# First pieces loaded in one go, and attention rows of the tail turned by VectorE instead of TensorE

## The reference

```python
x  = inputs                                  # (4, 1024, 256)
xn = layernorm(x)
# attention: 16 heads; the reshape takes heads along the sequence, then q, k, v are split
qkv = xn @ W_qkv + b_qkv                     # 256 -> 768
attn = softmax(mask(q @ k.T * 512 ** -0.5))
sa  = (attn @ v).reshape(4, 1024, 256)
out = sa @ W_out + b_out
# light network on every row: hidden 128; h = rms_norm(xn) * gamma_light
light = gelu(h @ w1_light + b1_light) @ w2_light + b2_light
# router: 50 iterations of coordinate descent on s = xn . routing_token, then top 256 of each batch
sel = top_k(exp((s + a + b) / 0.1), 256)
heavy[sel] = (gelu(rms_norm(xn[sel]) * gamma_heavy @ w1_heavy + b1_heavy) @ w2_heavy + b2_heavy) * gate
return x + out + light + heavy
```

## Time and profile before

| | before |
|---|---|
| median of 3 runs | 711.55 us (711.24 to 713.2) |
| profiled execution | 714.09 us, span 712.4 us |
| PE busy | 667.8 us (94%) |
| VectorE busy | 554.8 us (78%) |
| ScalarE busy | 403.5 us (57%) |
| GpSimd busy | 380.6 us (53%) |
| mean granted clock of PE | 0.982 |

### The profile page before, as it was taken

The page is one execution under the profiler, slowest core; times in us unless marked ns, Lnnn a source line. Parts: engine busy times, 40 slices in busy tenths (PEclk is TensorE's granted clock), DMA queues, the critical chain, the costliest instruction groups (busy, mean ns, idle before and its releaser), DMA issues. The chain is left out here.

```text
span 712.4 us, 12474 instructions
## 1 busy us (share of the span) xinstructions
PE 667.8 (94%) x3987; PEld 296.2 (42%) x3987; DVE 554.8 (78%) x1571; ACT 403.5 (57%) x908; POOL 380.6 (53%) x774
## 2 busy tenths in 40 slices
PE   4997999899999999899989999999999999999995
PEld 2653555333323333233323332333333436568665
DVE  4865888999999999999989999999998575152111
ACT  2332222787777777467768877777767554332320
POOL 4686130488775847857957853554442454413303
PEclk9999999999999999979999999999999999999998
DMA  8888996678949649696987944844833323442512
GB/s 276 207 219 196 242 264 179 154 141 129 180 70 161 129 63 163 103 132 111 152 160 99 164 73 52 120 75 51 174 63 29 121 60 92 147 148 88 119 59 30
DMA packets 247057, 92.49 MB, mean 130 GB/s; under 512 B 212992, under 2 KB 232608, under 8 KB 243872
## 3 DMA queue, kind: packets, MB, share of 16 engines
q1 hardware_dynamic: 245456, 89.60, 63.0%
q0 software_dynamic: 1536, 2.10, 1.8%
HBM read 56.65 MB, written 35.01 MB: 129 GB/s over the span
## 5 line engine op out<-in xcount | busy, mean ns | idle before, releaser
L1288 DVE CUSTOM_DVE_ANT_0 ps<-ps,maskrow 128x640 f32<-128x640 f32 (+7 forms) x512 | 375.3, 779 | 30.9 <-PE ps L1039 29.4
L897 ACT ACTIVATE strips<-ps 128x512 f32<-128x512 f32 (+1 forms) x608 | 313.2, 576 | 112.0 <-PE ps L1081 89.5
L1039 PE MATMUL ps<-QTk,QTq 96*128 96x512 bf16 (+3 forms) x768 | 189.2, 335 | 18.5 <-DVE mx L1288 10.6
L1081 PE MATMUL ps<-QTq,QTk 99*128 99x512 bf16 (+3 forms) x768 | 185.4, 331 | 2.8 <-DMA QTq<-m_d 1.9
L1099 PE MATMUL ps<-strips,vext 128*32 128x512 f32 (+3 forms) x1536 | 162.8, 500 | 0.9 <-DVE oT L1311 0.4
L1039 PEld LDWEIGHTS ps<-QTk,QTq 96*128 96x128 bf16 x768 | 53.3, 98 | 166.6 <-DVE mx L1288 133.1
L1081 PEld LDWEIGHTS ps<-QTq,QTk 99*128 99x128 bf16 x768 | 68.2, 98 | 89.3 <-ACT strips L897 41.2
L1739 POOL TENSOR_SCALAR_AFFINE_SELECT strips<-strips 128x512 f32<-128x512 f32 x128 | 79.3, 636 | 43.2 <-ACT strips L897 42.8
L999 PE MATMUL ps<-shared,xrT 128*128 128x384 f32 (+1 forms) x256 | 94.8, 503 | 0.2
L1288 DVE DVE_READ_ACCUMULATOR2_ANT mx<- 128x1 f32 x512 | 72.1, 141 | 0.0
L999 PEld LDWEIGHTS ps<-shared,xrT 128*128 128x128 f32 x256 | 47.3, 196 | 26.8 <-issue 3.1
(11 more groups left out here) (153 smaller groups left out, 689.8 us busy)
## 6 DMA issues: line engine op xcount, KB each, us to landing
pieces_d<-pieces SPq DMA_DIRECT2D x64, 192.0 KB, 3.4
qk<-qkv_d SPq DMA_DIRECT2D x64, 128.0 KB, 4.0
qkv_d<-shared SPq DMA_DIRECT2D x16, 384.0 KB, 3.8
QTq<-pieces_d SPq DMA_DIRECT2D x16, 384.0 KB, 5.2
QTk<-pieces_d SPq DMA_DIRECT2D x16, 384.0 KB, 7.7
vext<-qkv_d SPq DMA_DIRECT2D x16, 256.0 KB, 5.8
QTq<-pieces_d SPq DMA_DIRECT2D x16, 256.0 KB, 5.6
QTk<-pieces_d SPq DMA_DIRECT2D x16, 256.0 KB, 8.3
```

Source lines behind the costliest of these rows:

```text
L897: nc.scalar.activation(dst, src, ACT.Exp, scale=SCALE).then_inc(exp_done, 1)
L1039: mm = pe.matmul(psM[:, s, at:at + n], QTq[0:W, f % 3, c * 1024 + qb * P:c * 1024 + (qb + 1) * P], QTk[0:W, f % 3, c * 1024 + k0:c * 1024 ...
L1081: mm = pe.matmul(psE[:, (NE * q + j) % ES, k * n:(k + 1) * n], QTk[0:W + 3, q % 3, c * 1024 + kb * P:c * 1024 + (kb + 1) * P], QTq[0:W + 3 ...
L1288: ins = nc.vector.tensor_tensor_reduce(scores, scores, maskrow[:, 1024 - n:1024], 1.0, MASKED, ALU.add, ALU.max, mx[:, f % 2, 8 * c + qb:8 ...
```

## The change

It has two parts that don't touch each other.

In the projection, the transfers of the blocks' rows and pieces and of other data are put behind other tiles. Block 0's two piece loads are issued back to back; block 1's rows are loaded behind tile 10 instead of 5, its turn is at tile 13 instead of 10; block 2's turn is at tile 18 instead of 15; the value loads and the light weights are placed elsewhere.

In the tail, the attention rows are turned by VectorE (`turned`) in blocks of 32 x 32, two operations a unit, each of 128x512. A new view `sa_blocks` loads a unit's rows in four transfers with 256-byte rows, such that 32 x 32 blocks suffice, and W_out is loaded in the matching order of rows. `saT` holds a whole unit, twice. PE's transposes and ScalarE's copies go; `psC` has four banks; PE waits for a unit's turn at its first tile. On VectorE units (0, 0) and (0, 1) are turned ahead of the last item `("OT", 15, 1)`, and unit (i + 1, u) behind the evictions of unit (i, u) or soon after. In the heavy rows bias times gate is computed ahead (`heavy_bias`), and one operation is left behind the matmuls.

```diff
-    T_AT = {5: 0, 10: 1, 15: 2}
+    T_AT = {5: 0, 13: 1, 18: 2}
...
-                if t in (2, 5, 11, 16):
-                    load_qk((2, 5, 11, 16).index(t))
-                elif t in (4, 13):
-                    load_v(t // 10)
-                elif t == 20:
+                if t in (2, 10, 14, 20):
+                    load_qk((2, 10, 14, 20).index(t))
+                elif t in (26, 27):
+                    load_v((26, 27).index(t))
+                elif t == 16:
                     load_light()
-                elif t in (6, 15, 22):
-                    store_pieces((6, 15, 22).index(t))
-                elif t in (8, 17, 23):
-                    load_pieces((8, 17, 23).index(t), 0)
-                elif t in (9, 18, 24):
-                    load_pieces((9, 18, 24).index(t), 1)
+                elif t in (6, 17, 23):
+                    store_pieces((6, 17, 23).index(t))
+                elif t == 8:
+                    load_pieces(0, 0)
+                    load_pieces(0, 1)
+                elif t in (19, 24):
+                    load_pieces((19, 24).index(t) + 1, 0)
+                elif t in (21, 25):
+                    load_pieces((21, 25).index(t) + 1, 1)
...
+                for a in range(4):
+                    sp.dma_start(wout[32 * a:32 * a + 32, :, :], W_out.rearrange("(a k p) n -> a p k n", a=4, p=32)[a]
+                                 ).then_inc(wd_in, 16)
...
+            sa_blocks = sa_d.rearrange("(n m s) (a f) -> n a s m f", m=16, s=32, a=4)
...
-                sp.dma_start(sa_in[:, u], sb3[bass.ds(2 * i + u, 1)].rearrange("a p t e -> (a p) t e")).then_inc(c_in[u], 16)
+                for a in range(4):
+                    sp.dma_start(sa_in[32 * a:32 * a + 32, u].rearrange("p t e -> p (t e)").rearrange("p (m f) -> p m f", m=16),
+                                 sa_blocks[2 * i + u, a]).then_inc(c_in[u], 16)
...
-                o = psC[:, t % 2, 0:E]
+                o = psC[n % 4][:, 0:E]
...
+                if t == 0:
+                    pe.wait_ge(saT_done, KE * (2 * i + u + 1))
                 for k in range(KE):
-                    mm = pe.matmul(o, saT[:, t % 2, k * P:(k + 1) * P], wout[:, k, :], start=False, stop=(k == KE - 1))
+                    mm = pe.matmul(o, saT[u][:, k, t * P:(t + 1) * P], wout[:, k, :], start=False, stop=(k == KE - 1))
...
+            def turned(i, u):
+                dve.wait_ge(c_in[u], 16 * 4 * (i + 1))
+                if i > 0:
+                    dve.wait_ge(o_ps, 8 * (i - 1) + 4 * u + 4)
+                elif u > 0:
+                    dve.wait_ge(qk_ps, NE * NQ)
+                blocks = sa_in[:, u].rearrange("p t e -> p (t e)").rearrange("p (m k f) -> p k m f", k=KE, f=32)
+                for k in range(KE):
+                    nc.vector.transpose(saT[u][:, k, :].rearrange("p (m s) -> p m s", s=32), blocks[:, k]).then_inc(saT_done, 1)
+
+            last_outputs = ("OT", NQ - 1, 1)
             for item in order["Vector"]:
+                if item == last_outputs:
+                    turned(0, 0)
+                    turned(0, 1)
...
+            def heavy_bias(sts):
+                for st in sts:
+                    nc.vector.tensor_scalar(hv[:, st, :], bias_h, gw[:, st:st + 1], None, ALU.mult).then_inc(hb_done, 1)
...
-                    nc.vector.tensor_tensor(hv[:, st, :], psH[:, st % 2, 0:E], bias_h, ALU.add).then_inc(hv_half, 1)
-                    dve.wait_ge(hv_half, st + 1)
-                    nc.vector.tensor_scalar(hv[:, st, :], hv[:, st, :], gw[:, st:st + 1], None, ALU.mult).then_inc(hv_done, 1)
+                    nc.vector.scalar_tensor_tensor(out=hv[:, st, :], in0=psH[:, st % 2, 0:E], scalar=gw[:, st:st + 1],
+                                                   in1=hv[:, st, :], op0=ALU.mult, op1=ALU.add).then_inc(hv_done, 1)
...
             unit(0, 1, range(2, 4))
+            turned(1, 0)
+            turned(1, 1)
             gathered_invert(1)
             unit(1, 0)
+            turned(2, 0)
             gathered_normalise(1)
             gathered_gates()
             unit(1, 1)
+            turned(2, 1)
...
             unit(2, 0)
+            turned(3, 0)
             heavy_rows(range(2, 4))
             unit(2, 1)
+            turned(3, 1)
```

More of the change, by code:

```diff
@@ L386, in layer_kernel @@
     FIRST_DONE = FRONT_FROM + 2 * NU
-    T_AT = {5: 0, 10: 1, 15: 2}
+    T_AT = {5: 0, 13: 1, 18: 2}
     P_AT = {t + 2: f for t, f in T_AT.items()}
-    N_DCONST, N_CONST, N_FOLD = 2, 14, 5
+    N_DCONST, N_CONST, N_FOLD, N_WD = 2, 14, 5, 10
     N_SEARCH = 3
@@ L414, in layer_kernel @@
         psO = ps[:, 7]
-        psX = ps[:, 0:2]
         psG = ps[:, 6:8]
@@ L418, in layer_kernel @@
         psA = [ps[:, 4 + 2 * u:6 + 2 * u] for u in range(2)]
-        psC = ps[:, 4:6]
+        psC = [ps[:, b] for b in (0, 1, 4, 5)]
         psH = ps[:, 2:4]
@@ L536, in layer_kernel @@
         xgT = QTk[:, 0, :].bitcast(F32).rearrange("p (k n) -> p k n", k=KE)
-        saT = strips[:, 8192:8704].rearrange("p (b e) -> p b e", b=2)
+        saT = [y.rearrange("p (k n) -> p k n", k=KE) for y in (k_free[:, 3072:4096], QTq[:, 0, :].bitcast(F32)[:, 0:1024])]
         hot = [y.bitcast(BF16).rearrange("p (t n) -> p t n", n=NUM_HEAVY)
@@ L597, in layer_kernel @@
         h_done = sem("h_done")
-        saT_ps = sem("saT_ps")
         saT_done = sem("saT_done")
@@ L615, in layer_kernel @@
         ho_ps = sem("ho_ps")
-        hv_half = sem("hv_half")
+        hb_done = sem("hb_done")
         hv_done = sem("hv_done")
@@ L761, in load_bulk @@
                     sp.wait_ge(qkv_st[u], 16 * (NT // 4))
-                for dst, src in ((w2l, w2_l), (wout, W_out.rearrange("(k p) n -> p k n", p=P)),
+                for a in range(4):
+                    sp.dma_start(wout[32 * a:32 * a + 32, :, :], W_out.rearrange("(a k p) n -> a p k n", a=4, p=32)[a]
+                                 ).then_inc(wd_in, 16)
+                for dst, src in ((w2l, w2_l),
                                  (w2h, w2_h.rearrange("(k p) n -> p k n", p=P)),
@@ L832, in unit @@
                 if more:
-                    sp.wait_ge(saT_ps, 8 * i + 4 * u + 4)
+                    sp.wait_ge(saT_done, KE * (2 * i + u + 1))
                     load_sa(i + 1, u)
@@ L926, in hidden @@
                 nc.scalar.activation(hT[:, u, :], xrT[:, 0, 512 * (2 * i + u):512 * (2 * i + u) + 512], ACT.Gelu, bias=b1l[:, 0:1]).then_inc(h_done, 1)
[L928 to L937, removed]
             def gathered(h):
@@ L953, in _ @@
             hidden(0, 0)
-            unit(0, 0)
-            unit(0, 1)
+            hidden(0, 1)
             gathered(0)
+            hidden(1, 0)
             heavy_hidden(0, range(4))
-            unit(1, 0)
+            hidden(1, 1)
             heavy_hidden(0, range(4, NHC))
-            unit(1, 1)
+            hidden(2, 0)
             act.wait_ge(gu_done, 2 * NSLOT + 1)
             nc.scalar.activation(gscore[:, :], gu[:, :], ACT.Exp, scale=1.0 / EPS_ROUTE).then_inc(gs_done, 1)
-            unit(2, 0)
-            unit(2, 1)
+            hidden(2, 1)
             gathered(1)
+            hidden(3, 0)
             heavy_hidden(1, range(4))
-            unit(3, 0)
+            hidden(3, 1)
             heavy_hidden(1, range(4, NHC))
-            unit(3, 1, more=False)
         @block.tensor
@@ L1122, in _, with project_c @@
                     ring_item(item)
-            def transposes_c(i, u, t):
+            def project_c(i, u, t):
                 n = 8 * i + 4 * u + t
+                o = psC[n % 4][:, 0:E]
                 if t == 0:
[L1128 to L1132, removed]
+                    pe.wait_ge(h_done, 2 * i + u + 1)
+                if n == 0:
                     for x in slots[-MS:]:
@@ L1135, in transposes_c, with unit @@
                         pe.wait_ge(free[s], at + 1)
-                for k in range(KE):
[L1137 to L1141, removed]
-                o = psC[:, t % 2, 0:E]
[L1143 to L1155, removed]
-                    mm = pe.matmul(o, saT[:, t % 2, k * P:(k + 1) * P], wout[:, k, :], start=False, stop=(k == KE - 1))
+                    pe.wait_ge(wd_in, 16 * N_WD)
+                elif n == 2:
+                    pe.wait_ge(exp_done, NE * NQ)
+                if n >= 4:
+                    pe.wait_ge(ob_done, n - 3)
+                pe.matmul(o, hT[:, u, t * P:(t + 1) * P], w2l, start=True, stop=False)
+                if t == 0:
+                    pe.wait_ge(saT_done, KE * (2 * i + u + 1))
+                for k in range(KE):
+                    mm = pe.matmul(o, saT[u][:, k, t * P:(t + 1) * P], wout[:, k, :], start=False, stop=(k == KE - 1))
                 mm.then_inc(o_ps, 1)
-            def unit(i, u, more=True):
+            def unit(i, u):
                 for t in range(4):
[L1161 to L1164, removed]
                     project_c(i, u, t)
@@ L1196, in heavy_out @@
                     if st >= 2:
-                        pe.wait_ge(hv_half, st - 1)
```

(12 more changed lines are left out.)

2 lines of the change are left out of this document (1 added, 1 removed).

## The result

The changed kernel takes 707.44 us in the median of 9 runs (706.09 to 710.04); the kernel before, run beside it, 712.27 (711.24 to 713.93). The ratio is 0.9935, 95% interval 0.9921 to 0.995: 4.8 us faster, where 10.1 were forecast and 697 to 705.5 us given as the range.

A forecast was written before the change was run, and what follows sets the result against it. PE, busy 94% of the span, was taken to bound the kernel. The tail's -10.5 us and the projection's +0.4 gave -10.1 off the median of 711.55: 701.5 us, range 697 to 705.5.

The forecast's parts named there:

- The step that failed: Projection: PE waits 2 us for the first maximum behind the second block's turn, 0.9 late at its third score item.
- 0.5 of it: Projection: some 0.5 us of PE's delay comes back, as the third block's turn moves to tile 18, where VectorE is less behind.
- +0.4: Projection: net loss of 0.4 us from the new order of loads and turns, bounds -0.85 and +1.5.
- The bound of +1.5: Projection: upper bound of 1.5 us on the loss from the new order, whose forecast was +0.4.
- The tail: Behind the last step: 10.5 us gained, 10.1 from PE's transposes and unit-entry waits, 0.4 from bias times gate; bounds 8 and 11.
- The second load: Tail: the second load of gathered rows lands between 608.2 and 614.2, taken as 611, without holding up PE.
- A second half clock: Projection: PE's wait from 62 to 64 brings another half-clock stretch costing at most 1.7 us, 703.2; chance 20%.
- The front pays: Projection: the stall closes wholly, saving the 4.57 us gap and 1.7 of half clock, 694.7; chance 7%.
- turns in series: Tail: each of six later units waits for its own VectorE turn, 8.4 us back, 709.9, in part 704 to 707; chance 8%.
- Late keys: Projection: the second block's keys land at 107 when PE wants them at 104, losing 3 us, 704.5; chance 7%.

The follow-up runs named there:

- e2: The kernel before with only the projection's new order of loads and turns, its tail unchanged: 717.83 us, ratio 1.0075 to the kernel before.
- e4: The changed kernel with the second block's rows loaded behind tile 5 and turned in tile 10, as before: 701.68 us, ratio 0.9852 to the kernel before.
- e3: The changed kernel with the second block's turn in tile 15 instead of 13, its load still late: 703.01 us, ratio 0.9867 to the kernel before.
- e6: The changed kernel with the second block's rows loaded behind tile 5 instead of 10, turn still at tile 13: 703.65 us, ratio 0.9876 to the kernel before.
- e1: The changed kernel with the projection's lists of before, so the new tail alone: 701.54 us, ratio 0.9845 to the kernel before.
- e10: e5 with three added fp32 matmuls on PE ahead of the first scores, results overwritten: 699.71 us, ratio 0.983 to the kernel before.
- e11: e4 with five added fp32 matmuls on PE ahead of the first scores, results overwritten: 701.39 us, ratio 0.9854 to the kernel before.
- e5: e4 with the first block's turn at tile 4 instead of 5: 699.21 us, ratio 0.9825 to the kernel before.
- e8: e1 with the first block's turn at tile 4 instead of 5: 699.18 us, ratio 0.982 to the kernel before.
- e9: e4 with ten added fp32 matmuls on PE ahead of the first scores, results overwritten: 701.76 us, ratio 0.9856 to the kernel before.

## Why the prediction was wrong

**The step that failed**: "PE runs tile 14 from 57.1 to 62 and waits for 2 us: it is 0.9 late at that item". The words ahead of it take the score slots to be two, so that the first maximum holds up PE's third item, and it names the one that started at 63.17. But the table of slots is `place = {x: (0, n) for n, x in enumerate(FIRST)}`: in the projection every item uses slot 0. Two slots belong to the steps. So the first maximum holds up the *second* item, between the two halves of tile 14, and PE stands still from 59.2 to 63.8 instead of for 2 us. The third item came at 67.41, 15.1 us behind the pair of transposes instead of 10.1: 5.0 late, not 0.9. Of these, 3.85 are there at the second item (63.80 - 52.33 instead of 60.68 - 53.06), and the other 1.1 come between it and the third, at half clock. Nor did 0.5 of it come back: at the end of the projection it was 5.4. The term "+0.4" of the sum measures +5.4 in the profiles and +5.3 by e2; of the 5.3 us between the forecast's -10.1 and the measured -4.8 this is nearly all. The bound of +1.5 had no working beside it and fell with the term. That there is one slot is read from the code, and PE's wait for the first maximum ahead of the second item bears it out; no run gives the projection two.

**What that step rested on was near.** The changed kernel is 0.7 us earlier than the kernel before up to the pair of transposes, so forecast and measurement are compared from the pair on, which stood at 53.06 and stands at 52.33. The turn of the second block's rows was to begin 8.8 us behind it and began 9.4 behind; the first maximum was to end 11.0 behind and ended 11.4 behind (in the profile's own times the turn came at 61.72 for 61.9, which looks closer than the working was). First scores were to come 4.0 us behind the pair, a gap shorter by 0.9, and came 4.5 behind. Even this half microsecond is not clear of scatter: with the keys right behind the queries the first gap was 3.59 us (e4), 4.09 (after), 4.11 (e3), 4.48 (e6) and 4.53 (e2), with a store between them 4.57 (before) and 5.23 (e1). What I left out on the way is VectorE's eviction ahead of the turn: it waits for a store that now stands behind the keys (7.14 us, to 57.71). The load hid that here; it is the 0.7 to 1.1 us that e3, e4, e10 and e11 pay.

**The tail was right**: 10.5 forecast, 10.2 in the profiles (11.0 by e1's median). Units take 10.56 + 6 x 5.17 = 41.6 us (forecast 41.3), a unit's two turns 1.3 (1.4). No unit waits for its turn. The second load landed at 614.9, which is 17.6 us behind the tail's start at 597.35; 17.0 were forecast from a start at 594.00, between 14.2 and 20.2. It had no effect on PE, as forecast.

**The rivals.** *A second half clock* is half of the truth: the clock stayed down, for 10.2 us in the two kernels that have the long second gap (after and e2); it was priced at 1.7 and cost 1.1 more than before, the smaller part beside the gap itself. *The front pays* and *turns in series* did not come. *Late keys* did not either, and the reason I gave for and against was beside the point. SP's timeline has the issues, and the DMA view of 99 to 104.5 us what the last one took:

```profile
98.72 1.65 SPq L701 DMA_DIRECT2D QTk<-pieces_d  x3
```
```profile
QTk<-pieces_d SPq DMA_DIRECT2D x1, 128.0 KB, 6.3
```

They landed at 106.1, later than forecast (102); PE took them at 108.23. Each transfer stands behind a tile's store, and those move with PE, so a late PE finds them as it would in time: the slack is 2.1 us here, 2.2 in e3 and 2.3 in e5, whose PE takes them at 104.62 and 100.27.

## What to carry to other kernels

Ahead of reckoning what a late consumer costs, read from the code how many buffers the producer has in *that* stage; with one instead of two the wait falls one item earlier and takes the whole delay. An operation that is moved past others on an in-order engine must have its data by the time it stands there: the same turn cost 4.4 us with its load late (e3 against the change) and at most 2 with it landed (e6). And an exchange of work between a full engine and one with idle time could be priced from rows to a few tenths here, while a reordered queue is better tried alone.

## What was not expected of the hardware

PE's half clock was 3.41 us long behind a single wait of 4.57 (before), 1.98 (e5) or 3.53 us (e8), but 6.82 behind a single one of 5.23 (e1), where it began at 55.88, two microseconds ahead of the wait's end:

```profile
55.88:62.70 6.82, 4.87 (x10) 2.54 (x11) 1.70 (x3) 0.00 (x0) 6.54 (x50) 0.50 1.02 253
```

It was 6.8 us with a second wait of 0.68 (e3), 0.84 (e4) or 1.24 us (e6), and 10.2 with one of 4.30 (e2) or 4.59 (after). In the profiled executions of e11 and e10 waits of 1.47, 1.06 and 0.72 us between busy stretches brought none. So the length of a wait alone does not tell how long the clock stays down. The price was some 3.0 us in e4.

Nor had I expected the same key loads, in the same order, to land a microsecond apart.

The steps, the same instructions on PE in every kernel, take from 465.2 to 468.8 us in the profiles. The clock has a part in this: from 125 us to the tail it is at half for 17.07 us in before, after, e2, e3, e6 and e9, with PE busy 450.1 to 451.0, and for 10.24 us in the other six, with PE busy 448.0 to 448.2. The steps of before and of e8, columns as in the earlier trace rows:

```profile
125.19:594.00 468.81, 450.67 (x3132) 155.56 (x3133) 429.37 (x1236) 338.23 (x773) 289.68 (x604) 0.98 0.67 112
123.80:589.12 465.32, 448.01 (x3132) 154.89 (x3132) 431.68 (x1240) 338.36 (x774) 289.77 (x604) 0.99 0.68 112
```

Of the 3.5 us between these two, 2.7 are PE's longer busy time. Why the clock fell for longer in some kernels, and what makes the rest, was not tried and stays open.
